# The recurrence's x transposed by a DMA of 2-byte halves, in a three-layer decoder on one core

## The reference

```python
x = layernorm(x + self_attention(x))              # 16 heads, causal
x = layernorm(x + cross_attention(x, ctx_1024))   # ctx_1024: 16 x 750 x 512
x = layernorm(x + recurrence(x))

def recurrence(x):                                # c has the shape 224 x 512
    for xt in x:                                  # 16 steps, over the first axis
        ft = sigmoid(xt @ wf.T + c @ uf.T + bf)
        it = sigmoid(xt @ wi.T + c @ ui.T + bi)
        gt = tanh(xt @ wc.T + c @ uc.T + bc)
        c = ft * c + it * gt
    return tanh(x @ wo.T + c @ uo.T + bo)
```

## Time and profile before

| what | us |
|---|---|
| median of 3 runs | 1507.3 (1505.97 to 1507.41) |
| profiled execution, its own time | 1505.28 |
| profiled execution, span of the trace | 1503.1 |
| TensorE busy | 1449.2 (96%) |
| VectorE busy | 910.4 (61%) |
| ScalarE busy | 635.2 (42%) |
| GpSimd busy | 557.5 (37%) |
| cross-attention, one step | 29.25 |
| recurrence, one pair of blocks | 61.0 |

### The profile page before, as it was taken

The page is one execution under the profiler, slowest core; times in us unless marked ns, Lnnn a source line. Parts: engine busy times, 40 slices in busy tenths (PEclk is TensorE's granted clock), DMA queues, the critical chain, the costliest instruction groups (busy, mean ns, idle before and its releaser), DMA issues.

```text
span 1503.1 us, 28761 instructions
## 1 busy us (share of the span) xinstructions
PE 1449.2 (96%) x10322; PEld 1261.4 (84%) x10322; DVE 910.4 (61%) x1995; ACT 635.2 (42%) x1886; POOL 557.5 (37%) x431
## 2 busy tenths in 40 slices
PE   6999999999899999999999999999999999998797
PEld 3677777777689999999999889999999999987586
DVE  4578888888656656755665644345543554446487
ACT  4477777777344444344444413222222222221232
POOL 2455555554556565665656441000000000020254
PEclk9999999999999999999999997999999999998899
DMA  6123222324237533343343232000000010001353
GB/s 185 37 60 100 86 81 82 93 86 157 87 127 202 168 127 134 123 167 121 132 153 114 78 117 80 18 26 25 0 24 1 23 31 0 1 0 56 99 165 123
DMA packets 71611, 131.11 MB, mean 87 GB/s; under 512 B 7218, under 2 KB 15410, under 8 KB 71540
## 3 DMA queue, kind: packets, MB, share of 16 engines
q1 hardware_dynamic: 71540, 130.17, 27.1%
HBM read 106.30 MB, written 22.02 MB: 85 GB/s over the span
## 4 chain that ended last, share of the span: by engine, by line
PE 63%; issue 4%; POOL 3%; DVE 2%; ACT 0%; DMA 0%; SPq 0%; POOLq 0%; DVEq 0%
PE banks L1422 15%; PE banks L1441 10%; PE banks L928 8%; PE banks L913 8%; PE banks L942 6%; PE banks L900 5%; PE banks L1443 5%; PE banks L887 1%; POOL o_r L1934 1%; PE banks L1433 1%; PE banks L972 1%; POOL o_rstd L1942 1%; PE banks L1817 1%; PE banks L1406 1%; PE banks L879 1%
## 5 line engine op out<-in xcount | busy, mean ns | idle before, releaser
L433 ACT ACTIVATE s_p<-banks,a_nmax 112x224 f32<-112x224 f32 (+1 forms) x512 | 198.3, 416 | 94.7 <-DVE a_nmax L519 94.7
L697 POOL TENSOR_TENSOR s_p<-s_p,a_rinv 112x896 f32<-112x896 f32 (+1 forms) x128 | 164.8, 1309 | 167.2 <-DVE a_rinv L527 161.5
L1382 POOL CAST m_hi<-w_raw 128x2048 fp32r<-128x2048 f32 x1 | 1.9, 1896 | 434.0 <-PE banks L1422 434.0
L1612 DVE TENSOR_TENSOR f_gate<-banks,f_xg_early 128x448 f32<-128x448 f32 x45 | 28.1, 625 | 194.1 <-PE banks L1443 194.1
L1244 POOL TENSOR_TENSOR x_cx_lo<-s_cx_raw,x_cx_hi 125x512 fp32r<-125x512 f32 x96 | 120.6, 1295 | 66.2 <-ACT x_cx_hi L1042 66.2
L1528 ACT ACTIVATE f_gate<-f_gate 128x448 f32<-128x448 f32 x90 | 52.1, 579 | 187.8 <-DVE f_gate L1615 187.8
L534 DVE COPY a_pt<-banks 112x448 f32<-112x448 f32 x128 | 79.5, 621 | 62.4 <-PE banks L275 62.2
L1238 POOL TENSOR_TENSOR s_ct<-s_ct_raw,s_ct 128x750 fp32r<-128x750 f32 x60 | 111.3, 1885 | 11.0 <-ACT s_ct L1016 11.0
L433 ACT ACTIVATION_READ_ACCUMULATOR s_p<-banks,a_nmax 112x1 f32 x512 | 113.8, 222 | 0.0
L275 PEld LDWEIGHTS banks<-identity,s_p 112*112 112x112 f32 x768 | 86.1, 134 | 30.8 <-issue 9.3
L275 PE MATMUL banks<-identity,s_p 112*112 112x112 f32 x768 | 105.5, 261 | 0.9 <-DVE a_pt L534 0.9
(11 more groups left out here) (238 smaller groups left out, 3594.8 us busy)
## 6 DMA issues: line engine op xcount, KB each, us to landing
s_ct_raw<-in_ct SPq DMA_DIRECT2D x16, 1500.0 KB, 6.8
s_cx_raw<-in_cx SPq DMA_DIRECT2D x16, 1500.0 KB
a_xt<-in_xt SPq DMA_DIRECT2D x16, 448.0 KB, 3.9
a_xrow<-in_x SPq DMA_DIRECT2D x16, 448.0 KB, 3.6
a_xres<-in_x SPq DMA_DIRECT2D x16, 448.0 KB, 4.7
x_scratch<-a_xn SPq DMA_DIRECT2D x16, 448.0 KB, 3.1
x_scratch<-x_xn SPq DMA_DIRECT2D x16, 448.0 KB, 6.6
s_o_x_raw<-x_scratch SPq DMA_DIRECT2D x28, 256.0 KB, 2.8
```

Of the source, the lines that this page charges most:

```text
L433: e = act.activation((p1 if c else p0)[:, g, h, :], src, ACT.Exp, bias=nmax[:, g % 2, c, h:h + 1], accum_out=rsum[:, g % 2, c, h:h + 1])
L697: pool.tensor_tensor(p[:, g, :, :], p[:, g, :, :], inv, ALU.mult).then_inc(norm_done, 1)
```

## The change

Each block of x2 is written to HBM a second time, as 2-byte halves: GpSimd copies xn (112 x 2 x 512 float32, read as 2048 16-bit numbers per partition) to a tile `halves` in which the 512 low halves of a row stand together and the 512 high halves behind them (`separate`, one instruction per block, behind `cxl` in each step of cross-attention). SyncE stores `halves` to the new tensor x2_halves (448 rows of 1 KB per block) behind the store of xn, with a wait for `separate` between the two. The recurrence's loads become one DMA transpose per block, of 448 x 512 2-byte numbers, whose output is x2 transposed, with both halves of each number in place; ScalarE and VectorE read it from SBUF with one instruction each where two read PSUM. TensorE's `next_turn` and `x_turn` and their semaphores go. In the loop, GpSimd's waits for `norm` and for the previous store of `halves` stand ahead of the last `cxl` instruction. The row stores of x2 stay, for the output gate.

```diff
             def store(b):
                 sp.wait_ge(xn_done, TC * (b + 1))
                 sp.dma_start(x2[b].rearrange("(c p) d -> p c d", p=R), xn[:]).then_inc(stored, 16)
+                sp.wait_ge(halves_done, b + 1)
+                sp.dma_start(x2_halves[b].rearrange("(c p w) d -> p c w d", p=R, w=2), halves[:]).then_inc(halves_stored, 16)
...
-                sp.wait_ge(stored, 16 * (b + 1))
-                sp.dma_start(x1_raw[b][:], x2[b].rearrange("(c p) d -> p c d", p=R)).then_inc(opening.x2_in[b], 16)
+                sp.wait_ge(halves_stored, 16 * (b + 1))
+                sp.dma_start_transpose(opening.x2t[b][:].bitcast(U16), x2_halves[b]).then_inc(opening.x2_in[b], 16)
             for b in range(B - 3, B):
                 store(b)
             sp.wait_ge(stored, 16 * B)
+            sp.wait_ge(halves_stored, 16 * B)
...
-            def next_turn(b):
...
-                if isinstance(b, int) and b == B:
-                    next_turn(0)
...
-                if isinstance(b, int) and b == B:
-                    next_turn(1)
...
                 for j in range(XC):
                     wait(pool, cxh_done, XC * b + j + 1)
+                    if not isinstance(b, int) and j == XC - 1:
+
+                        wait(pool, xn_done, TC * (b - 1))
+                        wait(pool, halves_stored, 16 * (b - 2))
                     pool.tensor_tensor(cx_lo[:, j, :], cx_raw[:, j, :], cx_hi[:, j, :], ALU.subtract).then_inc(cxl_done, 1)
...
+            def separate(b):
+
+                if isinstance(b, int):
+                    wait(pool, xn_done, TC * (b + 1))
+                    wait(pool, halves_stored, 16 * b)
+                pool.tensor_copy(halves[:].rearrange("p c w d -> p c d w"), xn[:].bitcast(U16).rearrange("p c (d w) -> p c d w", w=2))\
+                    .then_inc(halves_done, 1)
...
                 if within(b, B):
                     cxl(b)
+                if within(b - 2, B):
+                    separate(b - 2)
                 if isinstance(b, int) and b == B:
                     next_weight(0)
                     next_weight(2)
...
                 if not (isinstance(b, int) and b in (2, 3)):
-                    wait(sp, xt_done, b - 1)
-                sp.dma_start(x2_raw[:, a, :, :], x2[b].rearrange("(c p) d -> p c d", p=R)).then_inc(x2_in[a], 16)
+                    wait(sp, xtl_done, b - 1)
+                sp.dma_start_transpose(x2t[:, a, :, :].bitcast(U16), x2_halves[b]).then_inc(x2_in[a], 16)
...
-            def x_turn(b, a):
...
             x_part(0, 1)
-            x_turn(2, 0)
-            x_turn(3, 1)
             u_part()
...
-                wait(act, xt_done, b + 1)
+                wait(act, x2_in[a], 8 * (b - a))
                 wait(act, xpart_done, (TILES // 2) * (b - a))
-                act.activation(xt_hi[:, 0:2, a, :], turned(b, 0), ACT.Copy)
-                act.activation(xt_hi[:, 2:4, a, :], turned(b, 2), ACT.Copy).then_inc(xth_done, 1)
+                act.activation(xt_hi[:, :, a, :], x2t[:, a, :, :], ACT.Copy).then_inc(xth_done, 1)
```

More of the change, by code:

```diff
@@ L732, in self_attention, with cross_attention @@
         return Stage(sync, tensor, scalar, vector, gpsimd)
[L735 removed]
+def cross_attention(nc, io, x1, x2, x2_halves, raw, raw_in, shared, opening, banks):
     with ExitStack() as ctx:
@@ L945, in out @@
                     mm.then_inc(out_done, 1)
-            def next_turn(b):
-                bank = (ps_h, ps_s)[b]
-                pe.wait_ge(opening.x2_in[b], 16)
-                if b == 0:
-                    pe.wait_ge(r_done, TC * (B - 1))
-                else:
-                    pe.wait_ge(ptl_done, B)
-                for k in range(KC):
-                    for q in range(TC):
-                        mm = pe.transpose(pair(bank, k)[:, q * R:q * R + R], x1_raw[b][:, q, 128 * k:128 * k + 128], identity[0:R, 0:R])
-                mm.then_inc(opening.xt_done, 1)
             def next_input(t):
@@ L1167, in norm @@
                 wait(dve, stored, 16 * b)
+                wait(dve, halves_done, b)
                 for c in range(TC):
@@ L1281, in cross_attention, with recurrence @@
         return Stage(sync, tensor, scalar, vector, gpsimd)
-def recurrence(nc, io, x2, identity, cc, raw, raw_in, opening, closing, banks):
+def recurrence(nc, io, x2_halves, identity, cc, raw, raw_in, opening, closing, banks):
     GATES = ("f", "i", "c")
@@ L1391, in tensor @@
         def tensor(pe):
-            def x_turn(b, a):
-                if not within(b, B):
-                    return
-                wait(pe, x2_in[a], 8 * (b - a))
-                if isinstance(b, int) and b == 3:
-                    pe.wait_ge(xtl_done, 2)
-                elif isinstance(b, int) and b == 2:
-                    pe.wait_ge(xg_done, OPEN)
-                elif a == 0:
-                    wait(pe, xg_done, (TILES // 2) * b)
-                else:
-                    wait(pe, xtl_done, b)
-                for k in range(KC):
-                    for q in range(TC):
-                        mm = pe.transpose(turned(b, k)[:, k % 2, q * R:q * R + R], x2_raw[:, a, q, 128 * k:128 * k + 128], identity[0:R, 0:R])
-                mm.then_inc(xt_done, 1)
             def x_part(pair, half):
@@ L1462, in pair_steps @@
                     c_gate(first, 0, 0)
-                    x_turn(first + 2, 0)
                     c_gate(first, 0, 1)
                     c_gate(first, 0, 2)
-                    x_turn(first + 3, 1)
                     if isinstance(i, int) and i == B // 2 - 1:
```

50 lines of the change are left out of this document (20 added, 30 removed).

## The result

The changed kernel is slower: 1637.3 us (median of 4 runs, 1635.6 to 1639.0) against 1507.4 (4 runs, 1506.0 to 1508.2). The ratio is 1.086, 95% interval 1.084 to 1.088. The forecast had the side right and the size wrong: 1521 with a range of 1498 to 1545, where +130 us was measured and +13.9 forecast.

The account below looks back on a forecast made before the run. TensorE's program order was taken to bound the kernel. The terms -9.9 (gain) + 18.5 (steps) + 3.7 (hand-over stall) + 1.6 (clock) gave +13.9 us on 1505.3, 1519.2, and 1521 as median; range 1498 to 1545.

Parts of the forecast that it names:

- What bounds the kernel: Whole kernel: TensorE, busy 1449.2 of 1503.1 us, sets the time; work removed or waits added in dense stretches count directly.
- The gain: Recurrence: removed `x_turn`s save 12 x 0.70 = 8.4 us in the pairs and 1.5 in blocks 2 and 3, together 9.9.
- The length S of `separate`: GpSimd, cross-attention and hand-over: one copy of 2048 numbers takes 3.25 us, ends 1.9 and 4.6.
- The law, a loss of S - 1.83 per step: Cross-attention: `separate` holds VectorE's second `shift`, so residuals and `zt` come late; 1.42 us per step, 18.5 in all.
- The count of 13: Cross-attention: the loss occurs 13 times, where `separate` stands ahead of a `zt`, behind steps 2 to 14.
- The clock: Cross-attention steps: TensorE's granted clock falling behind each new gap, left outside the range as part of a 0.1 chance.
- the last tenth: Outcomes beyond the range, 0.1 together: the long load's upper part and a granted clock falling in each step.
- The hand-over: Cross-attention to recurrence: queued loads move by 4.8 us, uf lands late, and TensorE stalls 3.7 us.
- The transposing load's time T: DMA queue ahead of uf at the hand-over: 3.6 us per load, ends 1.7 and 16.0; two add 3.8 us.
- The rival of the long load: Hand-over: a transposing load of 16 us stalls TensorE 28.5 us, giving 1546; range 1510 to 1550, chance 0.13.
- The clock at the hand-over: Before `out(15)`: idle time growing to 2.3 us lowers the granted clock, costing 1.6 us, ends 0 and 3.0.
- The rival of the short copy and short load: Copy takes 1.9 us, transposing load passes like plain rows, steps lose 0.9 us: 1498 to 1504, chance 0.32.

Follow-up runs that it names:

- Experiment 7: Changed kernel with `separate` writing densely, behind a wait for VectorE's `shift`, its store issued behind the next context load: 1495.2 us, ratio 0.9918 to the kernel before.
- experiment 2: Changed kernel with `separate`'s loops turned so that writes are dense and reads step; measured twice: 1497.8 and 1498.1 us, ratios 0.9946 and 0.9933 to the kernel before.
- experiment 1: Changed kernel with dense-writing copy plus small GpSimd operations in various read and write orders, put where GpSimd idles in the recurrence: 1496.6 us (one run).
- Experiment 3: Kernel before, plus only a slow-order GpSimd copy of half the numbers, 14 times, without stores or transposing load: 1551.7 us against 1505.5 (one run).
- experiment 8: Changed kernel with only block 0's copy made: 1504.7 us, ratio 0.998 to the kernel before; with that one copy written densely: 1496.9 us, 0.9928.
- experiment 6: Changed kernel, slow copy kept but waiting for VectorE's `shift`, its store issued behind the next context load: 1510.3 us, ratio 1.0023 to the kernel before.
- experiment 4: Kernel before, plus only a GpSimd memset of 2048 places in `separate`'s write order, 14 times: 1531.7 us against 1507.5 (one run).
- experiment 9: Changed kernel with the copy into halves made densely by ScalarE instead of GpSimd: 1500.3 us, ratio 0.995 to the kernel before.

## Why the prediction was right or wrong

- *What bounds the kernel: right.* Every wait put into a cross-attention step cost in full, and with the clock more than that, and what left the pairs was gained in full.
- *The gain: right, a little low.* 9.9 was forecast. A pair went from 61.0 to 59.4 us, so an `x_turn` is worth 0.77 us and not 0.70: 6 x 1.54 + 1.53 = 10.8. The 0.70 was the distance of two starts at one place; the length of the whole pair is the better measure. Experiment 7 has 11.9 us less behind the last `smax`; the 1.1 beyond these 10.8 isn't split, and kernels that differ little differ by as much there (638.0 to 641.0 in the table).
- *The length S of `separate`: the step that failed.* It was put at 3.25 with ends of 1.9 and 4.6 taken from the two nearest rows, and it is 9.42. The lower end holds for dense writes (1.90, experiment 2), the upper end was no bound at all: the subtraction of 4.6 us reads two tiles, and the number of operands has nothing to do with the order of the writes. The prediction saw that "no row shows such a write" and still closed the range with a row of another kind. It named the Trainium skill's section Memory Cachelines (page "Advanced Engine Details and Errata"), by which each access to a different 16-byte line is penalised. The direction is right for writes, 4.33 us against 0.94 for 768 numbers; for reads in the same order no penalty shows (0.91, experiment 1). With S = 9.42 the sum's own law gives 13 x 7.6 = 99 us in place of 18.5, and 80 of the 116 us that the forecast lacked are this one term; in the hand-over's working the same S adds 12 more (below). The upper end of the range had a slip of its own: the working gives 1541 for S = 4.6, not 1545.
- *The law, a loss of S - 1.83 per step: right, but for the clock and for one hold.* From 714.86, where the held addition ended, the exponential, `x1tl` and the residuals follow as written out, and `zt` starts 13.62 us behind the start of `separate` (719.67 - 706.05), where the law has 4.49 + 9.42 = 13.91. Experiment 3 has 3.3 against 3.0 at S = 4.87, half a microsecond less of waiting and the clock's part on top. That the held instruction was the addition ahead of the `shift` made no difference: both must be through before the exponential. The count of 13 left one out. `separate(13)` stands ahead of no `zt`, but the exponential of block 15 queues behind it all the same, and TensorE's last transposes of the softmax waited 5.28 us for it, at the granted clock of 0.50 again behind it:

```profile
985.43 2.86 PE L894 MATMUL banks<-identity,x_p 112*125 112x112 f32 x12 [5.28 <-ACT x_p L1037]
```

- *The clock: wrong in its place.* A fall of the granted clock in each step was put into the last tenth. It came every time, behind idle times of 4.60 to 4.75 us, and lasted until 6.5 to 10 us after TensorE had begun again. A step lost 9.2 where the idle time is 5.4, so 3.8 are the clock's, of which the law's 7.6 contains some (the transposes of the softmax at half rate lie inside VectorE's chain). Beyond the law's 98.7 the stretch has 119.4 - 98.7 = 20.7 us, 1.6 a step. This hung on S too: at S = 3.25 the residuals alone would have been waited for, 1.4 us.
- *The hand-over: right in kind, too small by the same S.* The stall in `x_part(0, 1)` behind the rounding of uf came where it was forecast, 7.4 us against 3.7. S stands in the working twice: with 9.42, `power(15)` is 1.1 + 9.42 - 3.03 = 7.5 late instead of 1.3, and the stall is 7.5 + 9.4 + 0.2 + 3.8 - 4.9 = 16.0. TensorE waited 12.0 in all, in two places, because a second wait had not been priced: `separate(14)` stands ahead of GpSimd's split of the weights, and at 9.5 us it makes `m_lo` late, for which TensorE's `next_input` waited 4.6 us. The prediction had followed this instruction to `power(15)` alone and not to the weights that it is also moved past. Timelines of POOL, PE and ACT there, which answer to the earlier trace rows:

```profile
998.26 9.49 POOL L1243 COPY x_halves<-x_xn 112x2048 uint16<-112x2048 uint16 x1 [1.10 <-DVE x_xn L1155]
1007.32 2.47 POOL L1250 CAST m_hi<-w_raw 128x2048 fp32r<-128x2048 f32 x1
```

```profile
1014.43 1.86 PE L964 MATMUL banks<-s_xt,m_hi 128*128 128x448 f32 x4 [4.61 <-POOL m_lo L1252]
...
1048.72 7.34 PE L1393 MATMUL banks<-s_xt,s_wc 128*128 128x448 f32 x24 [7.40 <-ACT f_xg_late L1481]
```

```profile
1046.24 1.91 ACT L1536 ACTIVATE f_uf_hi<-w_raw 128x2048 fp32r<-128x2048 f32 x1 [9.11 <-DMA w_raw<-in_uf_t]
```

- *The transposing load's time T: right as a landing time, too large as a term of the sum.* It was put at 3.6, and the section on DMA issues (median us from issue to landing) has 4.2:

```profile
f_x2t<-x_halves SPq DMA_TRANSPOSE x14, 4.2
```

  The sum charged 2 x (3.6 - 1.7) = 3.8 us for the two transposing loads ahead of uf. Before, uf is issued 1.2 us behind the first of the two loads (891.36 - 890.18) and lands 8.4 later; after, it is issued 3.8 us behind (1039.24 - 1035.41) and lands 7.0 later (the view of the instructions on `in_uf_t`):

```profile
DMA to landing us min/median/max: 7.0/7.0/7.0
```

  That is 10.8 us against 9.6, so the two loads cost uf 1.2 us and not 3.8.

  Of the two rules quoted from the Trainium skill, the one that has transposing DMAs as fast as regular ones (page "Advanced Engine Details and Errata", section X-Bar Transpose (TRN2)) is near, 4.2 against the 3.6 of the earlier trace rows. The Trainium skill's 1309 ns for each 128 x 128 block (page "VectorE: DVE Perf Modes", section The three transpose paths), an estimated 18.3 us, doesn't fit this load by a factor of four. The rival of the long load is out: experiments 7 and 8 stall 0.7 us and not at all.
- *The clock at the hand-over: 1.6 was forecast, nothing came.* `out(15)` waited 2.26 us in the changed kernel and in experiments 2 and 7, as the 2.3 of the prediction, and the clock granted over the 5 us behind that was 1.00 in all three. Only in experiment 8, where it waited 3.65 us, was it 0.61 for 4.4 us.
- *The rival of the short copy and short load (1498) describes experiment 2 to the microsecond.* It said that it decides from S below 2.3; the copy written densely is at 1.90, and the kernel at 1497.8. That it is so near is in part luck: the rival had a gain of 9.9 and 0.9 lost in the steps, the runs have 10.8 and 2.8 to 4.0. Of the changed kernel itself it was false.
- *What stays open:* the 22 us lost behind the last `smax` are known in two parts and not in each wait. Experiments 6 and 7 price the slow copy at the hand-over at 15.8 (16.8 in their traces). The changed kernel has 6.7 more there than experiment 6 (661.5 - 654.8); it has the fourteenth hold, with its wait of 5.28 us, and experiment 6 has not. Also open is why a held VectorE instruction sometimes gets in between two of GpSimd's (`s_dot` of 3.01 us in experiment 6) and sometimes waits for four of them (7.26 in experiment 4); gaps between GpSimd's instructions are the likely reason, only argued here.

## What to carry to other kernels

When an instruction is new to a trace, its order of writes counts as much as its number of elements: have the writes dense and let the reads jump, and don't close a range with a row that differs in another property. While a GpSimd instruction reads SBUF, a VectorE instruction with two operands from SBUF was held to its end, so place it where VectorE's next instructions read PSUM or one SBUF tile, and look again at what GpSimd does next. (One SBUF tile was no sure escape: in experiment 9 the two instructions of `norm`, which read one tile and per-row scalars, took 6.76 us beside GpSimd's split of a weight.) Then read SyncE's program for what is queued behind the store of the result: two lines moved were worth 115 us here.

## What was not expected of the hardware

- GpSimd's far 16-bit writes: 4.33 us for 768 numbers where the same numbers written half by half take 0.94; 9.4 us for 2048, for a memset just as for a copy. Alternating within 8 bytes costs nothing (0.83), nor do far reads (0.91). For 4-byte numbers it is 0.88 against 0.51 for 384.
- The hold is by reads: an addition of 112 x 1 numbers took 8.75 us beside a GpSimd copy, and 0.16 beside a memset of the same length and order.
- After 4.75 us without a matmul TensorE ran at the level of 1.2 GHz for 9.6 us in the step shown (6.5 to 10 in the others), and a step lost 3.8 us on the mean to that beside 5.4 of idle time. The page's row of granted clock in 40 slices (tenths of full speed, 40.9 us a slice) shows it as the eights and the seven of slices 13 to 27, through the steps of cross-attention that hold a `separate` and the hand-over (the page of before has 9 in all of these slices but slice 25, a 7; the two eights near the end it has too):

```profile
PEclk9999999999998889988998897889999999998899
```

- A DMA transpose of 448 x 512 2-byte numbers landed in 4.2 us, within 0.6 of a plain load of as many bytes, and the issue of the two at the hand-over occupied SyncE's queue for 3.8 us, where two plain ones took 1.1 before:

```profile
1035.41 3.78 SPq L1350 DMA_TRANSPOSE f_x2t<-x_halves  x2
1039.24 0.58 SPq L48 DMA_DIRECT2D w_raw<-in_uf_t  x1
```
